# Applying the leaf QR sweeps' rotations to the eigenvector rows by one scan on VectorE and five operations on GpSimd, in a graph-network kernel with its own eigensolver

## The reference, cut to what matters

```python
h = relu(einsum('ts,bsh->bth', adj, x @ Wg0 + bg0))
h = relu(einsum('ts,bsh->bth', adj, h @ Wg1 + bg1))
for p in range(1, 5):                       # windows of p nodes
    last = lstm_last(Wih[p-1], Whh[p-1], ..., windows(h, p))
    h = h.at[:, idx, :].set(last)
x = layernorm(x + h)
L_norm = d_inv_sqrt[:, None] * (diag(deg) - A) * d_inv_sqrt[None, :]
_, U = eigh(L_norm)
agg = einsum('mn,bnd->bmd', U.T, x)
x = layernorm(x + einsum('nm,bmd->bnd', U, relu(agg @ W1 + b1) @ W2 + b2))
```

## Time and profile before

| | |
|---|---|
| median of 3 runs | 5593.32 us (5592.66 to 5594.75) |
| profiled execution, its own time | 5595.16 us |
| profiled execution, span | 5593.4 us |
| VectorE busy | 4320.4 us (77%) |
| GpSimd busy | 1034.7 us (18%), of which the rotations (L316 to L318) 456.9 us |
| TensorE busy | 3424.7 us (61%) |

### The profile page before, as it was taken

The page is one execution under the profiler, slowest core; times in us unless marked ns, Lnnn a source line. Parts: engine busy times, 40 slices in busy tenths (PEclk is TensorE's granted clock), DMA queues, the critical chain, the costliest instruction groups (busy, mean ns, idle before and its releaser), DMA issues.

```text
span 5593.4 us, 78480 instructions
## 1 busy us (share of the span) xinstructions
PE 3424.7 (61%) x19256; PEld 2435.6 (44%) x19256; DVE 4320.4 (77%) x26692; ACT 983.0 (18%) x4375; POOL 1034.7 (18%) x3640
## 2 busy tenths in 40 slices
PE   6888888888787777777599455473121130330675
PEld 4566566666666666666465222221121120210343
DVE  7666667777788888888866999999878879799334
ACT  1111112222222222222111333331000000000011
POOL 1111111111111111000023677676200000000000
PEclk5555555555555555555567777786555555565588
DMA  2000000000000000000000000000000000000001
GB/s 61 1 1 1 1 1 1 1 1 1 1 1 1 1 1 1 1 1 1 1 1 1 1 1 1 1 1 1 1 0 0 0 0 0 0 0 0 0 0 30
DMA packets 20820, 17.58 MB, mean 3 GB/s; under 512 B 6545, under 2 KB 16785, under 8 KB 20369
## 3 DMA queue, kind: packets, MB, share of 16 engines
q1 hardware_dynamic: 20368, 12.65, 0.9%
HBM read 8.41 MB, written 4.20 MB: 2 GB/s over the span
## 4 chain that ended last, share of the span: by engine, by line
DVE 57%; PE 35%; issue 6%; ACT 1%; DMA 0%; DVEq 0%
PE bank L528 10%; PE bank L540 5%; PE bank L532 3%; DVE qp L1299 2%; PE bank L511 2%; DVE ycol L1005 2%; DVE qp L1287 2%; DVE dif L1683 2%; PE bank L523 2%; DVE ts L1037 1%; DVE tau_row L1021 1%; PE bank L572 1%; PE bank L571 1%; DVE jcol L1029 1%; DVE gated L1019 1%
## 5 line engine op out<-in xcount | busy, mean ns | idle before, releaser
L528 PE MATMUL bank<-lapw,hid 128*32 128x160 f32 (+3 forms) x10200 | 660.1, 421 | 59.7 <-DVE lapw L978 16.2
L260 POOL TENSOR_TENSOR sq<-hid,ltm 128x4 f32<-128x4 f32 (+3 forms) x510 | 100.0, 196 | 2304.7 <-DVE hid L1032 2253.8
L620 PE MATMUL bank<-hid,rows 128*128 128x512 f32 (+1 forms) x504 | 319.6, 801 | 310.1 <-ACT dif L401 309.4
L528 PEld LDWEIGHTS bank<-lapw,hid 128*32 128x32 f32 x10200 | 394.3, 162 | 184.8 <-DVE lapw L1040 82.7
L540 PE MATMUL bank<-xp,ones 128*128 128x1 f32 x1020 | 299.2, 362 | 278.8 <-DVE xp L1029 278.8
L538 PE MATMUL bank<-xp,ones 128*128 128x1 f32 x1020 | 299.1, 362 | 185.6 <-DVE xp L1011 185.6
L540 PEld LDWEIGHTS bank<-xp,ones 128*128 128x128 f32 x1020 | 255.6, 311 | 322.3 <-DVE xp L1029 322.3
L538 PEld LDWEIGHTS bank<-xp,ones 128*128 128x128 f32 x1020 | 255.6, 311 | 229.3 <-DVE xp L1011 229.3
L620 PEld LDWEIGHTS bank<-hid,rows 128*128 128x128 f32 x504 | 119.3, 243 | 502.0 <-ACT dif L401 334.1
L511 PE MATMUL bank<-xn,ones 128*128 128x2 f32 x1020 | 299.3, 363 | 18.6 <-DVE xn L958 17.6
L532 PEld LDWEIGHTS bank<-lapw,ident 128*128 128x128 f32 x956 | 240.2, 312 | 157.9 <-issue 157.9
(11 more groups left out here) (749 smaller groups left out, 8881.8 us busy)
## 6 DMA issues: line engine op xcount, KB each, us to landing
out_x<-xs SPq DMA_DIRECT2D x16, 256.0 KB, 3.3
lapw<-in_adj SPq DMA_DIRECT2D x1, 1024.0 KB, 5.6
bias_rows<-in_L_gnn_bg SPq DMA_DIRECT2D x8, 64.0 KB, 6.3
hid<-lz SPq DMA_DIRECT2D x32, 1.0 KB, 1.7
bias_rows<-in_L_gnn_b SPq DMA_DIRECT2D x4, 64.0 KB, 5.8
wg<-in_L_gnn_Wg SPq DMA_DIRECT2D x2, 64.0 KB, 5.1
wg<-in_L_gnn_W SPq DMA_DIRECT2D x2, 64.0 KB, 4.7
dif<-in_L_gnn_Wih SPq DMA_DIRECT2D x1, 0.5 KB, 7.4
```

What stands on the lines that cost most here:

```text
L528: m = pe.matmul(bank[1][32 * q:32 * q + 32, 0:(T + 1) * 32].rearrange("p (u i) -> p u i", i=32), acols[:, t, k:k + 1].to_broadcast([P, 32] ...
L620: m = pe.matmul(bank[4 * h + q][:, 0:cols_], wih_t[:, p - 1, q * P:(q + 1) * P], hid[:, b0:b0 + nb, t:t + (nw - 1) * p + 1:p], start=True, ...
```

## The change

The rotations of a sweep are applied to all 16 rows of a leaf at once. Written along the chain of rotations, what is carried from one rotation to the next is a first-order linear recurrence (the carried value times minus a sine, plus an element times a cosine). `lz` now holds, in each of 16 rows `r`, the 16 entries of that row in reverse order `j`. Per sweep GpSimd makes three operands (`near`: the entries times a cosine; `sines`: minus the sines copied to 16 rows; `far`: the entries times a sine), VectorE runs the recurrence over all 256 elements in one scan (`carry`), and GpSimd finishes with a product and a sum (`turned`). The new operands lie in tiles that are free in this stage (`vyrow`, `scrow`). `rot` has one more column, `zt` is gone. At the end GpSimd copies `lz`, reversed back, to `leaf_out` (in `pair`), from which the DMAs now read.

```diff
+        leaf_out = pair[0:LB, 0:P, :].rearrange("l (i a) b -> l i (a b)", i=LS)
+        near, far, run, sines = [q[0:LB, k * LS * LS:(k + 1) * LS * LS] for q, k in ((vyrow, 0), (vyrow, 1), (scrow, 0), (scrow, 1))]
...
-                sp.dma_start(vt[p0:p0 + LS, b * LS // P, b * LS:(b + 1) * LS], lz[b:b + 1, :, :]).then_inc(vt_in, 16)
+                sp.dma_start(vt[p0:p0 + LS, b * LS // P, b * LS:(b + 1) * LS], leaf_out[b:b + 1, :, :]).then_inc(vt_in, 16)
...
+            def turned(w):
+
+                pool.wait_ge(run_ready, w + 1)
+                pool.wait_ge(far_ready, w + 1)
+                pool.tensor_tensor(lz[:], square(run), rows_of(rot[:, w % 2, 0, LS - 1::-1]), ALU.mult).then_inc(turn_link, 1)
+                pool.wait_ge(turn_link, w + 1)
+                pool.tensor_tensor(lz[:, :, 0:LS - 1], lz[:, :, 0:LS - 1], square(far)[:, :, 1:], ALU.add).then_inc(rot_used, 1)
+                pool.wait_ge(rot_used, w + 3)
+
             for w in range(SWEEPS):
                 h = w % 2
+                if w:
+                    turned(w - 1)
                 if w + 1 < len(WINDOWS):
                     window(w + 1)
                 pool.wait_ge(rot_ready, w + 2)
-                for i in range(LS - 2, -1, -1):
-                    pool.tensor_scalar(zt[:, 0:2, :], lz[:, i:i + 2, :], rot[:, h, 0, i:i + 1], None, ALU.mult)
-                    link(pool.tensor_tensor(zt[:, 3:1:-1, :], lz[:, i:i + 2, :], rot[:, h, 1:3, i:i + 1].to_broadcast([LB, 2, LS]), ALU.mult))
-                    m = pool.tensor_tensor(lz[:, i:i + 2, :], zt[:, 0:2, :], zt[:, 2:4, :], ALU.add)
-                    if i:
-                        link(m)
-                m.then_inc(rot_used, 1)
-                pool.wait_ge(rot_used, w + 3)
-            pool.wait_ge(rot_ready, SWEEPS + 1)
-            pool.nop().then_inc(leaves_done, 1)
+                pool.tensor_tensor(square(near), lz[:], rows_of(rot[:, h, 0, LS:0:-1]), ALU.mult).then_inc(turn_in, 1)
+                pool.tensor_copy(square(sines), rows_of(rot[:, h, 2, LS:0:-1])).then_inc(turn_in, 1)
+                pool.tensor_tensor(square(far)[:, :, 1:], lz[:, :, 1:], rows_of(rot[:, h, 1, LS - 1:0:-1]), ALU.mult).then_inc(far_ready, 1)
+            turned(SWEEPS - 1)
+            pool.tensor_copy(leaf_out, lz[:, :, ::-1].rearrange("l r j -> l j r")).then_inc(leaves_done, 1)
...
+            def carry(w):
+
+                dve.wait_ge(turn_in, 2 * (w + 1))
+                V.tensor_tensor_scan(run, sines, near, 0.0, ALU.mult, ALU.add).then_inc(run_ready, 1)
+
             def rotation_block(n, w):
...
                 if n == 2:
                     mark(V.tensor_tensor(qt[:], qt[:], qh[:, 0:40], ALU.mult))
+                    if w:
+                        carry(w - 1)
...
             for n in range(M):
                 rotation_block(n, SWEEPS - 1)
                 since(cnt[0])
+            carry(SWEEPS - 1)
             dve.wait_ge(rot_ready, SWEEPS + 1)
```

More of the change, by code:

```diff
@@ L141, in program @@
         lz = sb("lz", [LB, LS, LS]); lzr = sb("lzr", [LB, LS, LS]); la = sb("la", [LB, 16, LS])
-        bh = sb("bh", [LB, 4]); lq = sb("lq", [LB, 32]); rot = sb("rot", [LB, 2, 3, LS])
+        bh = sb("bh", [LB, 4]); lq = sb("lq", [LB, 32]); rot = sb("rot", [LB, 2, 3, LS + 1])
         seen = sb("seen", [LB, LS + 1]); live = sb("live", [LB, LS + 1]); upd = sb("upd", [LB, LS]); sig = sb("sig", [LB, 1]); alt = sb("alt", [LB, LS])
         qa = sb("qa", [LB, 40]); qp = sb("qp", [LB, 100]); qi = sb("qi", [LB, 100]); qs = sb("qs", [LB, 40]); qh = sb("qh", [LB, 42]); qr = sb("qr", [LB, 40]); qt = sb("qt", [LB, 40]); was = sb("was", [LB, 2, LS]); qg = sb("qg", [LB, 8, LS]); qn = sb("qn", [LB, 2])
-        zt = sb("zt", [LB, 4, LS]); pause = sb("pause", [LB, 1]); spare = sb("spare", [LB, 4]); zero = sb("zero", [LB, 1])
+        pause = sb("pause", [LB, 1]); spare = sb("spare", [LB, 4]); zero = sb("zero", [LB, 1])
         hid = sb("hid", [P, B, N])
@@ L189, in program @@
         w_ready = sem("w_ready"); w2_ready = sem("w2_ready"); panx_ps = sem("panx_ps"); panx_sb = sem("panx_sb"); update_ps = sem("update_ps"); updated = sem("updated")
-        tri_link = sem("tri_link"); diag_in = sem("diag_in"); diag_ps = sem("diag_ps"); s_out = sem("s_out")
+        tri_link = sem("tri_link"); turn_link = sem("turn_link"); turn_in = sem("turn_in"); far_ready = sem("far_ready"); run_ready = sem("run_ready"); diag_in = sem("diag_in"); diag_ps = sem("diag_ps"); s_out = sem("s_out")
         block = ctx.enter_context(nc.Block())
@@ L248, in _ @@
             link(pool.memset(lzr[:], 0.0))
-            pool.memset(lz[:].rearrange("l i r -> l (i r)")[:, 0:LS * LS:LS + 1], 1.0)
-            link(pool.memset(lzr[:].rearrange("l i r -> l (i r)")[:, LS - 1:LS * LS - 1:LS - 1], 1.0))
-            link(pool.memset(zt[:], 0.0))
+            pool.memset(lzr[:].rearrange("l r j -> l (r j)")[:, 0:LS * LS:LS + 1], 1.0)
+            link(pool.memset(lz[:].rearrange("l r j -> l (r j)")[:, LS - 1:LS * LS - 1:LS - 1], 1.0))
             pool.memset(spare[:, 0:1], 0.0).then_inc(lz_clear, 1)
@@ L308, in window, with rows_of, square @@
                         lstm(job)
+            def rows_of(c):
+                return c.unsqueeze(1).to_broadcast([LB, LS, c.shape[-1]])
+            def square(q):
+                return q.rearrange("l (r j) -> l r j", j=LS)
+            def turned(w):
[5 more added lines that the diff above has]
+                pool.wait_ge(rot_used, w + 3)
             for w in range(SWEEPS):
                 h = w % 2
+                if w:
+                    turned(w - 1)
                 if w + 1 < len(WINDOWS):
@@ L1223, in rotation_block @@
                     mark(V.tensor_tensor(qg[:, 7, 0:M], qt[:, 20:20 + M], qg[:, 1, 0:M], ALU.mult))
-                    mark(V.copy_predicated(rot[:, h, 0, 0:M], was[:, 0, 0:M].bitcast(U32), qt[:, 0:M]))
+                    mark(V.copy_predicated(rot[:, h, 0, 1:1 + M], was[:, 0, 0:M].bitcast(U32), qt[:, 0:M]))
                 if n == 5:
-                    mark(V.copy_predicated(rot[:, h, 1, 0:M], was[:, 0, 0:M].bitcast(U32), qg[:, 7, 0:M]))
-                    mark(V.copy_predicated(rot[:, h, 0, 0:M], was[:, 1, 0:M].bitcast(U32), la[:, 6, 0:M]))
+                    mark(V.copy_predicated(rot[:, h, 1, 1:1 + M], was[:, 0, 0:M].bitcast(U32), qg[:, 7, 0:M]))
+                    mark(V.copy_predicated(rot[:, h, 0, 1:1 + M], was[:, 1, 0:M].bitcast(U32), la[:, 6, 0:M]))
                 if n == 6:
-                    mark(V.copy_predicated(rot[:, h, 1, 0:M], was[:, 1, 0:M].bitcast(U32), la[:, 7, 0:M]))
+                    mark(V.copy_predicated(rot[:, h, 1, 1:1 + M], was[:, 1, 0:M].bitcast(U32), la[:, 7, 0:M]))
                 if n == 7:
```

## The result

The kernel with the change takes **5627.3 us** (median of 4 runs, 5626.8 to 5630.6) against 5594.0 us for the kernel before in the same comparison (4 runs, 5592.7 to 5599.4): a ratio of 1.0059, 95% interval 1.0041 to 1.0076. It is slower by 33 us. The profiled execution took 5627.68 us, 32.5 more than the profiled one of before; its span is 32.5 us longer too.

A forecast was written before the change was run, and what follows sets the result against it. VectorE's instruction list was taken to bound 28 of the 36 leaf sweeps. Terms: -30.5 + 17.4 + 58.0 + 1.9 = +46.8 us on 5595.2, 5642, stated as 5640 us, slower by 0.8%; range 5600 to 5688.

The forecast's parts named there:

- the forecast's own case: Leaf sweeps: scan and five GpSimd operations cost more than the 45 small ones; 5640 us, bounds 5626 to 5665, chance 0.60.
- The rival at 5611: Leaf sweeps: only half the new GpSimd operations meet a blocked VectorE instruction; stall 1.03 us a sweep, +18 us, chance 0.13.
- What bounds the kernel, and GpSimd off the path: Leaf sweeps: VectorE's list sets the pace in 28 sweeps; GpSimd is never waited for and matters only by slowing VectorE.
- The 45 operations, 30.5 us gained: Leaf sweeps: removing the small GpSimd rotations gives VectorE back 1.10 us a sweep, 0.024 us each; 30.5 us gained.
- The scan, 17.4, and the end, 1.9: VectorE: one unhidden scan of 0.62 us in 28 sweeps, 17.4 us; lone scan and operand waits after the last sweep, 1.9.
- The five operations, 58.0: Leaf sweeps: four GpSimd products and a copy hold VectorE up 2.07 us in each of 28 sweeps, 58.0 us added.
- 0.28 us less than the instruction lasts: VectorE beside GpSimd: an operation is delayed by some 0.28 us less than the GpSimd instruction's duration, 0.99 against 1.286.
- The copy: GpSimd's one-input copy of 256 elements: bounded by 0 and 0.47 us of VectorE's time a sweep, taken as 0.25.
- Don't block: Rival, leaf sweeps: the new GpSimd operations don't block VectorE; -11 us, 5582, or 5585 at 0.024 us each; chance 0.11.
- They hold VectorE longer: Rival, leaf sweeps: new operations run 1.6 times longer, +103 us, 5696, or hold in full, +82, 5675; chance 0.16 together.
- The rule of the Trainium skill: VectorE and GpSimd share a port pair, held for whole instructions; the prediction priced stalls by the profile's rows instead.

The follow-up runs named there:

- kernel 2: The kernel before with each sweep's 45 rotation operations on GpSimd replaced by one small memset: 5562.0 us against 5593.3, ratio 0.9946.
- kernel 3: The changed kernel with its scan replaced by a one-column memset, GpSimd's five operations kept: 5608.4 us against 5593.3 for the kernel before, ratio 1.0027.
- kernel 8: The changed kernel with the copy of the sines moved from GpSimd to ScalarE: 5625.1 us against 5593.5 for the kernel before, ratio 1.0060.
- kernel 1: The kernel before, rotations kept, with a VectorE scan of 256 zeros added at the change's place: 5607.8 us against 5593.3, ratio 1.0026.
- kernel 12: The kernel before with each LSTM product on GpSimd cut into four pieces along its columns: 5535.6 us against 5594.1, ratio 0.9894.

## Why the prediction came out right, and which term was off

The forecast was 5640 us, the measured time is 5627.3: right in its direction and its mechanism, but at the low end of the forecast's own case (5626 to 5665). The rival at 5611 is not much farther off, so the time alone would not have told the two apart; the traces do.

**What bounds the kernel, and GpSimd off the path: right.** VectorE has no row of a wait for GpSimd in mid-sweep, ScalarE's `qr` waits for VectorE in the same 28 sweeps, and taking 12 us a sweep from GpSimd was worth 1.16.

**The 45 operations, 30.5 us gained: right**, 31.3 measured (kernel 2). Their price per operation, 0.024 us, was 0.026.

**The scan, 17.4, and the end, 1.9: right within 1 us.** The change's +33.3 less kernel 3's +15.1, each against its own kernel before, is 18.2 us. Kernel 3 keeps the last wait for the operands (1.35 us in its trace), which the prediction booked here, so 19.6 us stand against 19.3. Per sweep, the change against kernel 3 has 17.2 us over sweeps 9 to 34, 0.66 each. L1223 takes 0.67 us (0.69 on average with the long last one). One thing was forgotten at the end: two scans lie there, not one, since that of sweep 34 falls into the lone blocks. VectorE's timeline there:

```profile
3994.59 0.67 DVE L1223 TENSOR_TENSOR_SCAN scrow<-scrow,vyrow 32x256 f32<-32x256 f32 x1
...
3998.60 1.07 DVE L1223 TENSOR_TENSOR_SCAN scrow<-scrow,vyrow 32x256 f32<-32x256 f32 x1 [1.33 <-POOL scrow L334]
```

The last scan waits 1.33 us for its operands and is 0.40 longer than the others, since L335 is running when it starts; both were forecast. From the start of the last sweep to the end of the stage the kernel loses 4.4 us.

**The five operations, 58.0: this term was too large.** Kernel 3 has 46.4, and without the last wait, 1.35, the five cost 45.1. That is 12.9 of the 13.5 us by which the sum (+46.8) exceeds the measured +33.3; no other error had to make up for it. Two things are in it.

- *Their duration.* I took 0.73 us for all, from the rows of 512 and 340 elements. The rows have 0.726, 0.658, 0.673 and 0.624, and 0.387 for the copy. With the prediction's own "0.28 us less than the instruction lasts" these give 0.45 + 0.38 + 0.39 + 0.34 + 0.11 = 1.67 us a sweep; the windowless sweeps show 1.73 to 1.87, where the forecast had 2.07. So the rule was good and the lengths put into it were not. The copy was the largest guess: 0.25, against 0.08 by kernel 8.
- *The LSTM sweeps.* There the five cost 1.03 to 1.98 us, on average 1.49, because they also shift where VectorE meets the window's own products. Sweep 14 shows it: the change makes it only 0.64 us longer, while the lengthening of VectorE's instructions by its twelve products, summed over the timeline, falls from 12.45 to 11.88 us. Over sweeps 9 to 34 of kernel 3, against kernel 2, the instructions that the five operations meet are longer by 44.4 us in all, and what LSTM products add to theirs is less by 6.2. The forecast had one price for all sweeps.

The sum for sweep 33 closes with the scan's price from kernel 1: 24.86 - 1.16 + 1.73 + 0.58 = 26.01 us, against 26.00 measured. The forecast was 26.4.

**That it is all in held instructions** can be read from the timelines. Set each of VectorE's instructions in a sweep against the same one in kernel 2's windowless sweep, 23.70 us long, and add up what it takes longer. In the kernel before this gives 9.07 us in sweep 10, 13.62 in sweep 14, 6.24 in sweep 18 and 1.14 in sweep 33. With the 23.70 that makes 32.77, 37.32, 29.94 and 24.84, and the sweeps last 32.73, 37.27, 29.95 and 24.86. Each of the products in sweeps 10, 14 and 18 lengthens just one instruction, and that one ends within 0.03 us of the product. Nothing is left for another cause.

**The rivals.** "Don't block" falls by the timeline: five held instructions in each windowless sweep. "Only half of them meet a blocked instruction" (5611) falls too: all five meet one. "They hold VectorE longer" (5675 and 5696) falls by the durations, 0.62 to 0.73, and by the stalls. Rows of 16, read backwards or repeated, run no slower than the line says.

**The rule of the Trainium skill**, "SBUF — State Buffer", section "Who interferes with whom", that whoever starts first holds the shared port pair for its whole instruction: the trace agrees on the moment of release, within 0.02 us in the five cases above. But the hold is not the loss. What VectorE loses is what is left of the GpSimd instruction when the next instruction of VectorE that it blocks falls due. Between two of these in the recurrence lie instructions that it does not block, and latency; I read the 0.28 us as the mean part of a hold in which VectorE needs nothing. That is why pricing the new operations at their full duration (5675) was wrong, and why the small operations cost almost nothing without any exception to the rule: they too lengthen VectorE's instructions, by 0.1 us at most in sweep 33 and 1.14 in all. The 0.28 us is a property of this list of instructions, worked out from its rows; another kernel has another.

**Not settled.** Why the stages after the sweeps differ by up to 7 us between kernels that have the same code there; why sweep 6 takes one of two lengths; and, product by product, why the LSTM products and the rotations hold VectorE up for less when the scan (kernel 1, 0.48 instead of 0.58) or the five operations are added.

## What to carry to other kernels

Work moved to GpSimd beside a dense chain on VectorE is not free because GpSimd is idle: price it by how long its instructions hold VectorE up, and compare with what VectorE itself would need. Here four products of 256 elements cost VectorE as much on GpSimd as on VectorE, and the 128x512 products nearly twice as much (0.99 against 0.54 us), so the best version found takes those off GpSimd (5512 us, 1.5% below the kernel before). Where the work has to stay on GpSimd, many short instructions beat few long ones, as long as nobody waits for GpSimd: 45 operations became 5, and the kernel became slower. In kernel 12 GpSimd works 30.69 of 33.48 us, and VectorE still does not wait for it; how far this goes no run shows.
